# Macaron layer on one core: the second FFN block behind the context matmuls, Q and K projections one step later, statistics at other steps

## The reference

```python
def _conn_dense(kernel_bool, x):
    return x @ jnp.where(kernel_bool, 1.0, -1.0)

def _L0_ffn_ref(x, k0, k1, k2, s0, s1, s2):          # 256 -> 512 -> 512 -> 128
    h = jnp.concatenate([x, -x], axis=-1)
    h = jax.nn.relu(s0 * _conn_dense(k0, h)) * 2
    h = jax.nn.relu(s1 * _conn_dense(k1, h)) * 2
    return s2 * _conn_dense(k2, h)

def _L0_attn_ref(x, Wq, bq, Wk, bk, Wv, bv, gamma, beta):
    Q, K, V = ...                                    # x @ W.T + bias, by 16 heads
    attn = jax.nn.softmax(einsum('bhqd,bhkd->bhqk', Q, K) / sqrt(8), axis=-1)
    ctx = einsum('bhqk,bhkd->bhqd', attn, V).reshape(b, s, d)
    return _layernorm(ctx + x, gamma, beta)

x = x + 0.5 * ffn(_layernorm(x), ...)
x = x + attn(_layernorm(x), ...)
x = x + 0.5 * ffn(_layernorm(x), ...)
```

## Time and profile before

| | us |
|---|---|
| median of three executions | 778.4 |
| the three | 777.78, 778.40, 780.73 |
| the profiled execution | 780.73 |
| its span in the profile | 778.9 |

### The profile page before, as it was taken

How to read it: one execution, slowest core, us unless ns; L and a number is a source line. 1 busy time by engine, 2 the same in 40 slices (tenths; PEclk the granted TensorE clock), 3 DMA queues, 4 the chain that set the end, 5 groups by cost and what they waited for, 6 DMA issues and landing times.

```text
span 778.9 us, 18451 instructions
## 1 busy us (share of the span) xinstructions
PE 702.8 (90%) x7258; PEld 334.5 (43%) x7258; DVE 644.1 (83%) x1244; ACT 511.8 (66%) x736; POOL 369.5 (47%) x654
## 2 busy tenths in 40 slices
PE   6878497999999999999999999999999998787877
PEld 2433233444444444444444444444544444243334
DVE  5548768799998989898998989898999988677755
ACT  3324566777777777877777777778777776567642
POOL 4513234646463654646464636546364634625330
PEclk8788688999999999999999999999999999799998
DMA  3011001010201101010101011010202010010000
GB/s 71 15 47 49 16 2 64 2 63 16 64 16 43 36 13 53 16 63 16 64 15 63 17 42 37 3 63 16 63 16 63 15 51 16 2 62 3 15 2 27
DMA packets 29508, 25.62 MB, mean 33 GB/s; under 512 B 4336, under 2 KB 29424, under 8 KB 29424
## 3 DMA queue, kind: packets, MB, share of 16 engines
q1 hardware_dynamic: 28992, 24.07, 9.8%
q10 hardware_dynamic: 432, 0.39, 0.1%
HBM read 5.05 MB, written 4.19 MB: 12 GB/s over the span
## 4 chain that ended last, share of the span: by engine, by line
PE 62%; DVE 26%; ACT 5%; POOL 4%; issue 2%; DMA 0%; POOLq 0%; SPq 0%; DVEq 0%; ACTq 0%
PE ps_z L639 13%; DVE row_max L1320 12%; PE ps_z L640 12%; PE ps_c L802 9%; PE ps_s L751 8%; DVE ffn_lo L1210 7%; PE ps_m L725 4%; PE ps_m L814 2%; PE ps_z L650 2%; PE ps_z L623 2%; PE ps_z L652 2%; PE ps_m L736 2%; ACT probs L1013 2%; ACT ffn_hi L975 2%; DVE k_lo L1311 1%
## 5 line engine op out<-in xcount | busy, mean ns | idle before, releaser
L1320 DVE TENSOR_REDUCE row_max<-ps_s 128x4 f32<-128x1024 f32 x256 | 312.3, 1220 | 54.2 <-PE ps_s L751 53.2
L1013 ACT ACTIVATE probs<-ps_t,score_scale 128x1024 f32<-128x1024 f32 x252 | 280.2, 1112 | 74.3 <-PE ps_t L764 71.9
L975 ACT ACTIVATE ffn_hi<-ps_z 128x512 f16<-128x512 f32 x270 | 155.2, 595 | 95.3 <-PE ps_z L640 73.2
L639 PE MATMUL ps_z<-ffn_hi,w 128*128 128x512 f16 x480 | 184.8, 385 | 0.8 <-DVE ffn_lo L1210 0.6
L640 PE MATMUL ps_z<-ffn_lo,w 128*128 128x512 f16 x480 | 183.7, 383 | 0.0
L1210 DVE SCALAR_TENSOR_TENSOR ffn_lo<-ps_z,ffn_hi 128x512 f16<-128x512 f32 x240 | 161.4, 682 | 20.7 <-ACT ffn_hi L975 18.8
L802 PE MATMUL ps_c<-probs,v_cols 128*32 128x256 f32 x2048 | 133.6, 390 | 1.1 <-ACT probs L1013 0.7
L751 PE MATMUL ps_s<-k_rows,q_rows 32*128 32x256 f16 x1024 | 103.3, 280 | 31.6 <-DVE row_max L1320 27.9
L764 PE MATMUL ps_t<-q_rows,k_rows 32*128 32x256 f16 x992 | 99.6, 279 | 0.0
L751 PEld LDWEIGHTS ps_s<-k_rows,q_rows 32*128 32x128 f16 x1024 | 29.3, 93 | 123.4 <-DVE row_max L1320 62.0
L802 PEld LDWEIGHTS ps_c<-probs,v_cols 128*32 128x32 f32 x2048 | 57.4, 111 | 55.7 <-issue 28.4
(11 more groups left out here) (178 smaller groups left out, 1060.7 us busy)
## 6 DMA issues: line engine op xcount, KB each, us to landing
x<-L_attn_x SPq DMA_DIRECT2D x16, 256.0 KB, 2.7
q_rows<-q_hi SPq DMA_DIRECT2D x32, 128.0 KB, 2.5
y<-x SPq DMA_DIRECT2D x16, 256.0 KB, 2.1
k_rows<-k_hi SPq DMA_DIRECT2D x30, 128.0 KB, 2.1
q_rows<-q_lo SPq DMA_DIRECT2D x16, 128.0 KB, 2.1
q_rows<-no_max SPq DMA_DIRECT2D x16, 128.0 KB, 2.1
k_rows<-k_lo SPq DMA_DIRECT2D x15, 128.0 KB, 2.1
q_rows<-max_rows SPq DMA_DIRECT2D x64, 8.0 KB
```

Source lines behind the costliest of these rows:

```text
L639: pe.matmul(o[:], w, ffn_hi[:, 1 + k, :], start=(k == 0), stop=False)
L975: a_.activation(ffn_hi[:, use, :], ps_z[use % 2][:], ACT.Relu if use else ACT.Copy, scale=1.0 if use else XN_SCALE).then_inc(z_hi, 1)
L1013: a_.activation(probs[n % PROBS][:, j:j + 2, :], o[:], ACT.Exp, scale=score_scale[:, 0:1]).then_inc(s_exp, 1)
L1320: v.tensor_reduce(row_max[hb % 2][:].rearrange("p (a l) e -> p l a e", a=2)[:, j:j + 2, :, g % 2], ps_s[:].rearrange("p l (a k) -> p l a k ...
```

## The change

Three tables and one condition change.

- In a step, only piece 0 of an FFN now comes ahead of the contexts. Before, piece 3 (block 1 of the first layer) did too. Piece 3 falls into steps 3 and 19, in both of which a context group and a transpose of row maxima stand.
- Q goes from step 8 to 9 and K from step 11 to 12, on all engines.
- The aggregates of `AT_STATS_A` go from step 10 to 9. The four bn_stats of `AT_STATS_PREP` go from steps 18, 18, 20, 20 to 20, 22, 26, 28, their aggregates from 26 to 29.

```diff
--- before.py
+++ after.py
@@ -47,7 +47,7 @@
 
 
 
-AT = {"LNT": 6, "Q": 8, "K": 11, "CT0": 14, "CT1": 22, "V": 25}
+AT = {"LNT": 6, "Q": 9, "K": 12, "CT0": 14, "CT1": 22, "V": 25}
 AT_ALONE = {"CT0": 7, "LNT": 11, "Q": 14, "K": 17, "CT1": 22, "V": 30}
 AT_ZERO = {"LNT": 2, "Q": 4, "K": 6, "V": 8}
 AT_OWN_LAST = {"CT0": 7, "CT1": 19}
@@ -63,14 +63,13 @@
 SPREADS_FIRST = 4
 PROBS = 6
 WARM_UP = 16
-AT_STATS_A, AT_STATS_B, AT_STATS_PREP = ((2, 2, 3, 3), 10), ((24, 24, 25, 25), 27), ((18, 18, 20, 20), 26)
+AT_STATS_A, AT_STATS_B, AT_STATS_PREP = ((2, 2, 3, 3), 9), ((24, 24, 25, 25), 27), ((20, 22, 26, 28), 29)
 AT_STATS_A_ALONE = ((2,) * TT, 3)
 AT_STATS_B_ZERO, AT_STATS_PREP_ZERO = ((28,) * TT, 29), ((25,) * TT, 31)
 AT_STATS_SOLO = (27, 28)
 AT_STATS_TAIL, AT_STATS_TAIL_ALONE, AT_STATS_TAIL_EARLY = (18, 30), (11, 28), (11, 22)
 
 
-FIRST_IN_STEP = (0, 3)
 FFN_IN = {2: 0, 3: 1, 4: 2, 5: 3}
 FFN_MID = tuple((6 + n, 2 * n, 2 * n + 2) for n in range(8))
 FFN_MID_DONE = {7: 0, 9: 1, 11: 2, 13: 3}
@@ -871,7 +870,7 @@
                     lanes(it, s)
                     pieces = [(f, piece) for f, _, piece in ffn_work(it, s)]
                     for f, piece in pieces:
-                        if piece in FIRST_IN_STEP:
+                        if piece == 0:
                             ffn_piece(f, piece)
                     tile, parity, groups = contexts(it, s)
                     for g in groups:
@@ -890,7 +889,7 @@
                         if s == at(it, "V"):
                             project_v(it.misc["V"])
                     for f, piece in pieces:
-                        if piece not in FIRST_IN_STEP:
+                        if piece:
                             ffn_piece(f, piece)
                     if it.prep:
                         if s == at(it, "Q"):
```

## The result

| | us |
|---|---|
| before, median of 4 executions (777.78 to 780.73) | 779.37 |
| after, median of 4 executions (788.18 to 790.81) | 789.9 |
| ratio after / before, 95% interval | 1.0107 (1.0081 to 1.0135) |
| profiled execution of after: time, span, mean granted clock | 787.64, 785.8, 0.963 |
| profiled execution of before | 780.73, 778.9, 0.956 |

The changed kernel is slower. The forecast was 788.6 with a range of 782 to 795. More executions narrow the two medians: the 61 of before that ran beside the experiments have a median of 779.4 us, and all 24 of after on record, the four above among them, one of 788.0 (784.9 to 790.8). So the change costs 8.6 us rather than the 10.5 of the first four; the two profiled spans are 6.9 us apart.

What follows compares the result with a forecast made beforehand. TensorE was taken as the bound, busy 41.72 of 43.00 us an iteration, with a few joints where VectorE decides. 12 x 0.42 + 13 x 0.40 = 10.2 us on the median of 778.4 gave 788.6, range 782 to 795.

Steps and rivals of the forecast that it cites:

- the joints: TensorE's stops for ffn_lo (L650), k_lo (L814) and row_max (L751), where VectorE decides: 1.27 us an iteration.
- (a): Rival: ScalarE's 0.67 us delay is absorbed, leaving only 0.06 us gained, 13 times: 777.6 us; chance 0.11 with what lies near.
- (b): Rival: TensorE's idle 0.41 us ahead of L814 is gained in 13 halves, 5.3 us faster; chance 0.06.
- (c): Rival: the clock falls, one more stretch at 0.88 giving 794 us; chance 0.05, shared with delays larger than predicted.
- Part 1, first half: Steps 18 to 24: block 1 behind the contexts makes L639 0.25 us late.
- Second half: Steps 2 to 8: block 1 behind the contexts makes L639 in step 6 0.46 us late.
- only 0.14 and 0.07 of room stand in the rows: Second half: ScalarE's next split absorbs 0.14 us of the delay, and the second layer's ffn_lo answer 0.07 more.
- the walk: The prediction's row-by-row following of delays through one iteration: 43.00 us becomes 43.82; chance of 784 to 793 us 0.76.
- GpSimd's answer: Max transposes in the second half: TensorE starts 0.05 us after GpSimd's max_parts ends.
- high bound: GpSimd's answer 0.1 us longer (1.3 us), first iteration and last tiles 1 us each: 13.5 us, 792.
- Part 2 in company: Step 30: a bn_stats and aggregates, 0.59 us against 0.42 of room, make the row maximum 0.17 us later.
- Part 3: Second half, L814: Q and K one step later, k_lo at 372.01 against 372.07, 0.06 us gained.

Runs made afterwards that it cites:

- parts 2 and 3: Two runs on the kernel before: only the four bn_stats and their aggregates moved, 778.23 us; only Q, K and the step-10 aggregates moved, 779.99 us.
- part 1 alone: The kernel before with only block 1 of the first FFN layer put behind the contexts and max transposes: 787.86 us, ratio 1.0112.
- Part 2 alone: The kernel before with only the bn_stats moved to steps 20, 22, 26, 28 and their aggregates to 29: 778.23 us, single execution.
- CT0 alone: The kernel before with the first context transpose at step 15 instead of 14: 780.56 us, single execution.
- CT0 with the low part first: The kernel before with the first context transpose at step 15 and piece 13's ffn_lo ahead of the row maximum of steps 14 and 30: 775.06 us, ratio 0.9952.

## Why the prediction came out as it did

**What held.** The bound and the joints; the order of the parts, with block 1 carrying it; parts 2 and 3 worth nothing alone (0.04 and -0.04 us an iteration). Rivals (a) and (b) didn't come about, nor did (c): the clock stays at 1.00 in the loop. VectorE isn't idle before the maximum of step 30 and waits for k_hi ahead of k_lo (0.72 us), as asked.

**What was mis-sized: the loop, 6.9 us for 10.2.** Three terms.

*Part 1, first half: 0.25 predicted, 0.04 in the change and 0.18 alone.* *Second half: 0.46 predicted, 0.33 alone.* The failing step is the room on ScalarE, "only 0.14 and 0.07 of room stand in the rows". ScalarE's second split is late as read (360.31 - 1.55 = 358.76, the walk had 358.68). But the operations behind it take less from start to start than they did: the copy of 360.80 hands over to the exponentials after 0.26, where before has 0.37 (358.51 to 358.88), and the context copy of 362.06 to the next split after 0.26, where the walk took 0.34 (its 0.38 less 0.04). The 0.37 held a wait that the view doesn't print. In before the exponentials started 0.46 behind the shifted scores:

```profile
358.42 0.28 PE L764 MATMUL ps_t<-q_rows,k_rows 32*128 32x256 f16 x2
358.88 1.11 ACT L1013 ACTIVATE probs<-ps_t,score_scale 128x1024 f32<-128x1024 f32 x1
```

It is 0.46 to 0.47 in steps 2 and 6 of before as well, and 0.85 here in after (360.21 to 361.06), where ScalarE's own queue decides. So the next pair of splits starts at 362.32 - 1.55 = 360.77, which is 0.39 late and not 0.53, and in the first half at 340.92 - 1.28 = 339.64, 0.25 late and not 0.47. In the first half VectorE decided already in before, and the bn_stats that the change takes away from there gives back about 0.20, so that the ffn_lo is on time.

*And the path was another.* The walk carried the delay over the splits of blocks 2 and 3 to their ffn_lo and L638. It missed that in step 4 the row maximum stands behind block 1's own ffn_lo. Before:

```profile
338.69 1.22 DVE L1320 TENSOR_REDUCE row_max<-ps_s 128x4 f32<-128x1024 f32 x1
...
359.13 0.67 DVE L1210 SCALAR_TENSOR_TENSOR ffn_lo<-ps_z,ffn_hi 128x512 f16<-128x512 f32 x1
359.72 1.22 DVE L1320 TENSOR_REDUCE row_max<-ps_s 128x4 f32<-128x1024 f32 x1
```

There the ffn_lo of block 1 starts at 359.13 and the maximum behind it at 359.72. After (VectorE's rows above), that ffn_lo waits 0.17 for ScalarE and starts at 360.93 - 1.55 = 359.38, the maximum at 359.99, 0.27 late, and the scores of step 6 wait for it. They start at 362.82 - 1.55 = 361.27, against 360.99: 0.28 late. The wait ahead of them has grown by 0.04 only, from 0.21, since TensorE itself comes 0.24 late: the scores of step 4 start at 360.20 - 1.55 = 358.65, against 358.41. Of this 0.13 is the wait for max_parts, and 0.11 is that one more 512-column matmul is followed by another kind (0.31 from start to start where another of its kind takes 0.22). It is the busy time that the iteration has more. The walk had worked out block 1's start on TensorE but not carried it on to the scores of step 4. By itself TensorE's 0.24 would have cost 0.03, behind the old wait of 0.21; with the maximum 0.27 late it costs all. At L638 it is 363.67 - 1.55 = 362.12, against 361.81: 0.31 late. In the first half the same maximum is 0.17 late (340.14 - 1.28 = 338.86, against 338.69). The walk's road and this one lead to nearly the same place, which is why its sign and its order of size survive.

*GpSimd's answer, 0.15 for 0.05.* In the second half this cuts the other way: the transposes, and block 1 behind them, are 0.08 later than the walk had them (359.46 - 1.55 = 357.91, against 357.83). The high bound had it ("0.1 longer, 1.3 us").

*Part 2 in company: 0.17 predicted, 0.23 there.* VectorE in steps 28 to 30 of after, answering to the later rows:

```profile
349.97 1.23 DVE L1319 TENSOR_REDUCE row_max<-ps_s 128x4 f32<-128x1024 f32 x1
...
351.71 0.28 DVE L1291 BATCH_NORM_STATS2 att_bn<-x 128x6 f32<-128x128 f32 x1
352.09 0.38 DVE L1192 BATCH_NORM_AGGREGATE att_mv<-att_bn 128x2 f32<-128x6 f32 x4
352.39 1.19 DVE L1319 TENSOR_REDUCE row_max<-ps_s 128x4 f32<-128x1024 f32 x1
```

The bn_stats at 351.71 and the aggregates 0.38 later, not 0.31, then 0.30 to the maximum of step 30 at 352.39: 0.68 where the walk had 0.59. That maximum is 352.39 - 1.28 = 351.11, against 350.81: 0.30 late, although the one of step 28 (349.97 - 1.28 = 348.69, against 348.66) is only 0.03 late. TensorE's scores of step 30 are only 0.05 late (351.70 - 1.28 = 350.42, against 350.37), so 0.25 of it is the statistics'. With the aggregates at step 31 this goes, and the first half by TensorE's scores loses 0.05. With part 1 alone it is otherwise: the first half has +0.18, all of it from step 20 on. Part 2 alone has the maximum of step 28 0.19 early and that of step 30 0.08 late, and gives +0.04. So part 2 in company does both: it takes back what part 1 costs at step 20, and puts its own delay in at step 30. The walk's addition was right in form, with 0.25 + 0.17 in place of 0.04 + 0.23.

*Part 3: -0.06 predicted, about -0.04.* K's row in after ends the second half's +0.33 at +0.28. The two matmuls of block 1 start 0.23 us apart in after (359.66, 359.89), those of before 0.22. The rule of the Trainium skill that was weighed ("TensorE: Matmul & The Clock Gate", section "Back-to-back issue gap") has 0.131 for such a matmul in a sustained stream; the measurement decides.

**Right for partly the wrong reason: the ends.** The forecast carried its 10.2 us to the median and set nothing for head and tail, except in the high bound (1 us each). The 25 halves gave 6.9 us by the walk's count, and the medians of the long series differ by 8.6, so 1.7 us came from elsewhere: from the head, as far as the runs tell, or from the clock. The first four executions of after were on the high side of their own spread by some 2 us; their median of 789.9 lies 1.3 above the forecast. By the long series the forecast was 0.6 us high: by a loop 3.3 too dear and ends 1.7 too cheap, on a median of before that was 1.0 too low. That is luck in part. The forecast's last line had named time from the clock or from the first and last tiles as right for the wrong reason; for this part of the 8.6 us it is so.

**What stays open.** Where in the head its 1 to 2 us arise wasn't followed row by row, and they rest on a fit and on single traces at like clocks. That the order costs anything in the tail is not shown.

## What to carry to other kernels

An engine with a quarter of its time free (ScalarE, 31.7 of 43 us) may still sit on the path of the busiest one, if its queue is in order and hands something over in each step: delay one item and follow everything queued behind it, on every engine, up to the first instruction that the busiest engine waits for. Moved work inherits the dependences of what it is put behind (here block 1 came to depend on GpSimd). Two edits in one stretch can nearly add up in the time (0.18 and 0.04 us alone, 0.27 together) though neither delay stands where it stood alone, so read the stretch again with both in it. A wait removed shows up at the next joint: CT0 alone gave 0.03 us an iteration, CT0 with the low part first 0.34. And before a stretch at head or tail is put down to an edit, set it beside one of the old order at the same granted clock.

## What the runs showed of the hardware

- The start of a small ScalarE operation behind another is no sure measure of what it takes: a 16x256 copy and a 128x256 copy, of 0.36 us each, hand over after 0.26 (360.80 to 361.06, 362.06 to 362.32) when the next one waits for nobody. In before the first had 0.37 (358.51 to 358.88), with the exponentials behind it waiting for the scores without a printed gap.
- TensorE starts 0.15 us after the end of a GpSimd row it waits for (359.31 to 359.46; in the run with the aggregates at step 31, 360.74 + 0.22 = 360.96 to 361.11), and 0.05 after one of VectorE.
- bn_aggr behind the bn_stats that it reads starts 0.38 us after it (351.71 to 352.09), while bn_aggr behind one that it doesn't read starts after 0.20 (349.34 to 349.54 in after).
- The tail's time goes with its granted clock: 123.9 to 124.6 us at 0.94 and 125.4 to 126.2 at 0.93, over eleven traces.
- The same program's executions lie up to 0.75% apart, and the granted clock goes with it: after takes 784.9 to 785.9 us at a mean clock of 0.969 and 790.6 to 790.8 at 0.952. Four executions of each are not enough to settle 2 us.
